# The prologue of a graph network layer: first tile's statistics ahead of the edge search, SyncE issuing its moves, search groups of 20 targets instead of 10

## The reference, cut to what matters

```python
h = jnp.maximum(_layernorm(x, axis=-1), 0.0)
agg = segment_sum(edge_attr_64, dst, 50000)
counts = segment_sum(ones, dst, 50000)
agg = agg / jnp.maximum(counts, 1.0)[:, None]
combined = jnp.concatenate([agg, h], axis=1)
out = x + relu(combined @ W1 + b1) @ W2 + b2
```

## Time and profile before

| what | value |
|---|---|
| median of 3 runs | 1390.73 us (1389.94 to 1390.91) |
| span of the profiled execution | 1387.8 us |
| TensorE busy | 98% of the span |
| VectorE busy | 92% |
| ScalarE busy | 59% |
| GpSimd busy | 52% |
| chain that ended last | PE 97% |

### The profile page before, as it was taken

The page is one execution under the profiler, slowest core; times in us unless marked ns, Lnnn a source line. Parts: engine busy times, 40 slices in busy tenths (PEclk is TensorE's granted clock), DMA queues, the critical chain, the costliest instruction groups (busy, mean ns, idle before and its releaser), DMA issues.

```text
span 1387.8 us, 31376 instructions
## 1 busy us (share of the span) xinstructions
PE 1356.9 (98%) x6882; PEld 1099.1 (79%) x6882; DVE 1276.5 (92%) x3267; ACT 818.9 (59%) x1672; POOL 727.1 (52%) x1004
## 2 busy tenths in 40 slices
PE   3899999999999999999999999999999999999998
PEld 1688888888888888888888888888888888888887
DVE  6789999999999999999999999999999999999996
ACT  3556565656566565656565656565666656565653
POOL 4554545555555555554545454555555555555451
PEclk7999999999999999999999999999999999999999
DMA  5575757576666666575757575766666666757572
GB/s 101 104 142 107 144 107 139 110 137 112 134 114 132 117 130 124 122 132 114 142 105 144 107 140 109 137 112 135 113 133 116 131 120 126 130 116 137 109 129 56
DMA packets 424646, 168.87 MB, mean 122 GB/s; under 512 B 323181, under 2 KB 424247, under 8 KB 424633
## 3 DMA queue, kind: packets, MB, share of 16 engines
q1 hardware_dynamic: 421348, 166.77, 62.7%
q10 hardware_dynamic: 3284, 1.97, 0.8%
HBM read 66.07 MB, written 51.20 MB: 85 GB/s over the span
## 4 chain that ended last, share of the span: by engine, by line
PE 97%; DVE 1%; DMA 1%; ACT 0%; POOL 0%; issue 0%; ACTq 0%; DVEq 0%; POOLq 0%
PE P L852 26%; PE P L832 13%; PE P L854 13%; PE P L834 13%; PE P L833 13%; PE P L842 7%; PE P L841 7%; PE PS L811 3%; PE PA L821 2%; DVE below L627 1%; DMA HQ<-HN 0%; DMA dst_a<-in_dst_dram 0%; DVE HT L667 0%; ACTq L256 0%; ACT HN L514 0%
## 5 line engine op out<-in xcount | busy, mean ns | idle before, releaser
L852 PE MATMUL P<-w_both,H_hi 128*128 128x512 f32 x1568 | 566.7, 399 | 0.1
L550 ACT ACTIVATE H_hi<-P 128x512 fp32r<-128x512 f32 x392 | 234.8, 599 | 381.1 <-PE P L842 380.5
L854 PE MATMUL P<-w_both,H_lo 128*128 128x256 f32 x1568 | 438.1, 279 | 0.0
L852 PEld LDWEIGHTS P<-w_both,H_hi 128*128 128x128 f32 x1568 | 294.3, 188 | 67.3 <-DVE H_lo L684 0.5
L832 PE MATMUL P<-HT_hi,w_hi 128*128 128x512 f32 x784 | 325.7, 415 | 16.4 <-DVE HT_lo L675 16.4
L406 POOL TENSOR_TENSOR XB<-X,b_row 128x1024 f32<-128x1024 f32 x98 | 235.0, 2398 | 198.3 <-DVE O L695 198.3
L834 PE MATMUL P<-HT_hi,w_lo 128*128 128x512 f32 x784 | 311.0, 397 | 0.0
L833 PE MATMUL P<-HT_lo,w_hi 128*128 128x512 f32 x784 | 310.6, 396 | 0.0
L684 DVE SCALAR_TENSOR_TENSOR H_lo<-P,H_hi 128x512 fp32r<-128x512 f32 x392 | 268.7, 686 | 32.6 <-ACT H_hi L550 19.7
L854 PEld LDWEIGHTS P<-w_both,H_lo 128*128 128x128 f32 x1568 | 294.5, 188 | 4.2
L667 DVE STREAM_TRANSPOSE HT<-HQ 128x512 f32<-128x512 f32 x196 | 212.7, 1086 | 18.4 <-DMA HQ<-HN 18.1
(11 more groups left out here) (73 smaller groups left out, 1512.4 us busy)
## 6 DMA issues: line engine op xcount, KB each, us to landing
X<-in_x_dram SPq DMA_DIRECT2D x98, 512.0 KB, 4.5
HQ<-HN SPq DMA_DIRECT2D x388, 128.0 KB, 4.1
out_dram<-O SPq DMA_DIRECT2D x97, 512.0 KB, 4.4
ER<-in_edge_attr_dram SPq DMA_DIRECT2D x392, 32.0 KB, 1.8
DW<-in_dst_dram SPq DMA_DIRECT2D x392, 0.5 KB, 1.9
w_raw<-in_L_gnn_W_dram ACTq DMA_DIRECT2D x4, 128.0 KB, 7.6
w_raw<-in_L_gnn_W_dram ACTq DMA_DIRECT2D x2, 256.0 KB, 8.2
HQ<-HN ACTq DMA_DIRECT2D x4, 128.0 KB, 4.8
```

Of the source, the lines that this page charges most:

```text
L550: act.activation(H1_hi[:, m, :], bank(m)[:], ACT.Relu).then_inc(s_1hi, 1)
L852: pe.matmul(out_bank(j)[:], H1_hi[:, m, rows], w2_both[:, m, :, :].rearrange("p a d -> p (a d)"), start=(m == 0), stop=False)
L854: last = pe.matmul(out_bank(j)[:, 0:D], H1_lo[:, m, rows], w2_both[:, m, 0, :], start=False, stop=(m == CH - 1))
```

## The change

On SP the load of the first tile's `X` is issued ahead of `dst_a`, and SP issues the four moves of tile 0, before it waits for `s_start`. On ACT `layernorm(0)` stands ahead of the five casts, and ACT issues no moves. On DVE the statistics of tile 0 stand ahead of the search instead of behind its first part. `GR` is 20 instead of 10, so that there are 10 groups and not 20.

```diff
-    EP, GR = 125, 10
+    EP, GR = 125, 20
...
+            load_x(0, 0)
             sp.dma_start(dst_a[:], dst.rearrange("(p r) -> p r", p=EP)).then_inc(s_dst, 16)
-            load_x(0, 0)
             sp.wait_ge(s_zero, 1)
...
             load_x(1, 1)
+            move(0, 0)
             sp.wait_ge(s_start, 1)
...
+            layernorm(0, 0)
             act.wait_ge(s_w[0], 16 * QN)
             act.activation(w1_hi[:], w1_raw[:], ACT.Copy).then_inc(s_whi, 1)
...
             act.activation(w2_both[:, :, 0, :], w2_raw[:], ACT.Copy).then_inc(s_whi, 1)
-            layernorm(0, 0)
-            act.wait_ge(s_ln, SUB)
-            into_quadrants(act, 0)
             layernorm(1, 1)
...
+            stat(0, 0, range(SUB))
+            aggregate(0, 0)
             dve.wait_ge(s_dst, 16)
             dve.tensor_copy(lasts[:], dst_a[:].rearrange("p (g r) -> p g r", r=GR)[:, :, GR - 1]).then_inc(s_srch, 1)
...
             dve.tensor_reduce(fall[:], falls[:], AX_X, ALU.max).then_inc(s_fall, 1)
 
-            stat(0, 0, range(SUB))
-            aggregate(0, 0)
             found = PS[:].rearrange("p a b -> p (a b)")
```

## The result

The changed kernel takes 1434.9 us (median of 5, 1430.14 to 1438.28), the kernel before in the same comparison 1390.91: a ratio of 1.031, 95% interval 1.029 to 1.033, or 44 us slower. The forecast was 1388.9, and rival 4, the slower one, said 1394.

The account below looks back on a forecast made before the run. PE's unbroken work was taken as the bound, so only its start could move. Flag 1.0 + SP's windows 0.8 + slack 0.4 - clock 0.4 = 1.8 us: 1390.73 becomes 1388.9 us, range 1387.0 to 1390.8.

Parts of the forecast that it names:

- rival 4: Prologue: `dst_a` lands late behind X, at 15.05 us, delaying the flag 4.5 us; 3.3 us slower, 1394.0 us; chance 0.05.
- the first: PE's stretch from 120 to 700 us, busy 580.00 of 580 us: the prologue can only move it forward, not shorten it.
- a limit of 108: Search with groups of 20: `longest` may reach 128 - 20 = 108, so the general way stays untaken.
- L: Landing of tile 0's `X`, issued at 0.95 us: forecast 7.85 us, bounds 6.05 to 8.75.
- `dst_a`: Its load, now behind X in the queue: landing forecast at 9.2 us, before DVE is free for the search at 9.6.
- The flag: End of the search, for which SP waits: up at L + 9.93 = 17.8 us against 18.78, 1.0 us earlier.
- "3.12": Term of the flag's forecast: us from `start_f` to the end of `flag_i`, 18.78 - 15.66 in the trace before.
- SyncE's windows: SP's `ER` loads behind the flag: 1.60 us apart instead of 2.39 without ACT's moves, giving 0.8 us back.
- PE's start: PE's first matmul, behind `layernorm(1)` on ACT: forecast at 26.6 us, 4.1 us earlier.
- Where the lines meet: Tile 0's step: DVE waits for tile 2's `X` and `DW`; `rel` moves 2.2 us earlier, including 0.4 us of slack.
- The clock: PE's stretch at 0.50 clock may fall partly behind the new start, 46.9 us: 0.4 us charged, bounds 0 and 1.7.
- The gain: Whole kernel: 1.8 us faster, median 1388.9 us; bounds -1.2 and 4.0 us.

Follow-up runs that it names:

- e12: The kernel before with HQ alone, the destination of the moves, shifted by 32 bytes: 1435.96 us, ratio 1.032.
- e1: The changed kernel with 9,824 unused bytes per partition behind `below`, so the buffers behind it lie where they lay before the change: 1390.28 us, ratio 0.9998.
- e4: The kernel before in its old order, with groups of 20 instead of 10: 1428.48 us, ratio 1.028.
- e3: The changed kernel with groups of 10 again, so the new order alone with every buffer where it was before: 1394.62 us, ratio 1.003.
- e9: The kernel before with 64 unused bytes per partition behind `below`, putting the streamed buffers at multiples of 256 bytes: 1385.38 us, ratio 0.9960.
- e8: e1 with GpSimd's low part of W1 made only after the flag and that of W2 behind `norm(1)`: 1388.78 us, ratio 0.9986 to the kernel before.
- e11: The kernel before with HN alone, the source of the moves, shifted by 32 bytes (HQ by 256): 1390.54 us, ratio 0.9998.
- e5: The changed kernel with 160 unused bytes per partition behind `below`, putting the streamed buffers at multiples of 256 bytes: 1386.97 us, ratio 0.9966 to the kernel before.
- e6: The kernel before with HN and HQ shifted by 32 bytes, buffers ahead in place, those behind shifted by 256: 1438.23 us, ratio 1.034.
- e7: The kernel before with X, XB, O and what lies behind HQ shifted by 32 bytes, HN and HQ keeping their remainder by 256: 1392.25 us, ratio 1.0011.
- e10: e8's order on GpSimd with e5's places, buffers at multiples of 256 bytes: 1384.11 us, ratio 0.9953 to the kernel before.

## Why the prediction was wrong

**The step that failed** is the first: "A change to the prologue cannot shorten that; it can only move it forward." It took the stretch from 120 to 700 us as fixed, and with it the durations of the transfers. But the diff also resized two buffers, and the buffers behind them moved. HQ, whose 256-byte pieces had begun at multiples of 64 bytes, now begins 32 bytes off. e12 makes that one shift in the kernel before and gets 1436.0; e1 undoes all shifts in the changed kernel and gets 1390.3; e4 and e3 put it on the line of the group size and not on the order. The group size was costed as ten compares and a limit of 108, its buffers not at all, and no rival covered it: rival 4 put the loss in the landing of `dst_a`.

**Why half a microsecond per tile costs 44 us.** The page of before held the warning: transposes waiting 18.1 us in all on the moves, in small portions. The round from transpose to transpose was as long as PE's 13.7 us for a tile: the transposes started on average 0.10 us after their moves had landed. A longer move could hide nowhere. The last move took some 0.55 us longer, 0.08 of it came out of that slack, and the mean round grew by 0.49 us. Over 97 tiles that is some 47 us, and the spans of the two profiled executions differ by 47.6 (1435.4 and 1387.8; the medians by 44). It is also the difference between 2,961 and 2,874 matmuls in 580 us. With the buffers at multiples of 256 bytes the transposes start 1.2 us after the landing, and behind the prologue none waits for a move (e9).

**The prologue's own steps**, which e1 isolates, since it is the changed kernel without the shift:

- L: 8.54 us instead of 7.85, within the bounds of 6.05 to 8.75. From issue to the first statistics are 7.6 us, which is 0.2 less than the 7.8 before and not 0.9; why `dst_a`'s 98 KB going ahead had cost so little is open.
- `dst_a`: right; the first compare follows the statistics at once, at 10.45.
- The flag: L + 9.93 would be 18.5; it came at 20.24. The missing 1.7 us are one term, "3.12" from `start_f` to the flag, carried over from a trace in which the cast (16.79 to 17.19) and `reach` were done before GpSimd's subtraction for W1 began at 17.69. The new order puts GpSimd's subtraction for W1 (16.04 to 18.39) beside the cast to `start_i`, which took 2.11 instead of 0.40 us. e3 shows the same with another operation and GpSimd's other subtraction; e8 removes the overlap and the cast is back at 0.40, the flag at 18.29. The Trainium skill, page "Advanced Engine Details and Errata", section "Mode Summary" under VectorE's performance modes, says that VectorE's second port to SBUF is shared with GpSimd, and that GpSimd's instructions and those of VectorE that use both ports block each other. The cast agrees with that, at 2.11 us beside the subtraction and 0.40 without it; that `reach`, held up as well, uses both ports in that sense no run shows.
- SyncE's windows: 1.70 and 1.61 us between the first `ER` instead of 1.73 and 2.39, as forecast (0.8 us).
- PE's start: 27.94 us, behind `layernorm(1)` on ScalarE, as forecast but 1.3 later, since `norm(1)` now waits for the second statistics, which stand behind the late flag.
- Where the lines meet: right as to the wait. VectorE waits 1.24 us for X of tile 2 and 1.28 for its `DW`. In e1 the flag is 1.5 us later than before, 0.75 come back in SyncE's windows and 0.4 from the slack; that leaves `rel` 0.3 late by the sum, and it starts at 47.53, 0.36 later than in the earlier trace rows. The time is the same as before within the interval.
- That the flag's line sets the time agrees with three kernels with equal places: 18.29, 20.26 and 24.63 us at the flag (e8, e1, e3) give 1388.8, 1390.3 and 1394.6 us. PE's first layer of tile 1 starts at 50.96, 53.01 and 57.38 us in them, and at 52.75 before. PE's own start does not order them: it is 28.37 us in e8 and 27.96 in e1.
- The clock: the stretch at 0.50 came later, as feared. In e1 it holds from 46.2 to 49.5 us, so the prediction's sign "low for long after 47 us" came up. What it costs there is open. At its old place it cost nothing, though 1.7 us had been the price of a whole one: in e9, whose prologue is that of before, the clock was 1.00 from 43.70 to 47.10 us, but PE was busy for only 2.44 of the 3.40 us, and the first layer of tile 1 started at 52.92.
- The gain: e8, with both surprises out, gains 2.0 us where 1.8 were forecast. That is in part luck: its flag came 0.5 us earlier than before and not 1.0, and its order on GpSimd is not that of the change.

## What to carry to other kernels

A change of a buffer's size is also a change of where every buffer behind it lies; look at the starts of the buffers that transfers of small pieces write, and pin them to multiples of 256 bytes instead of leaving them to what is declared ahead. Where an engine waits in small portions for the same transfer in half of the steps of a loop, the loop may be bound twice; a bound engine at 100% does not mean slack in the round beside it. When a step is moved, price it with what runs beside it in its new place, on VectorE and GpSimd above all.

## What the runs showed of the hardware that was not expected

- The start of the destination in SBUF matters for DMAs with pieces of 256 bytes. The last of a tile's four moves landed after 3.2 us with the buffers at multiples of 256 bytes, after 4.3 with HQ at 192 beyond one (a multiple of 64), and after 4.8 with HQ at 96 or 224 beyond (32 beyond a multiple of 64). Other remainders were not tried. The source did not matter between 192 and 224 beyond (e11); a source alone at a multiple of 256 was not tried, so which side gives the 3.2 us is open. The Trainium skill, page "DMA: Bandwidth & Descriptors", section "How a descriptor splits into AXI transactions", says that a transaction must start at a multiple of 256 bytes, and that a descriptor which starts elsewhere has bytes fetched that are not used; it says this of reading. By that rule, as an estimate, a piece of 256 bytes takes two transactions wherever it starts between two such multiples, and one at a multiple. The 3.2 us of e5 and e9 agree with it. But a start at 192 and one at 224 would then both take two, and e12 against before shows 45 us between them, so something more counts, and what it is stays open.
- Other transfers on the same DMA engines pay with it: X took 5.0 us in e6 and e12 at its old place, and 4.5 in e7 at a shifted one.
- VectorE's cast of 0.40 us and its `reach` of 0.55 us took 2.11 and 2.69 us beside GpSimd's subtraction of 128x1024, and ended 0.3 and 0.4 us after it. `end_f`, which reads PSUM, kept its 0.55 us beside it. It works the other way too: in e3 GpSimd's subtraction for W1, begun amid VectorE's compares, took 4.66 us instead of 2.35 and ended 2.5 us after the last of them.
- With the buffers at multiples of 256 bytes PE also did 2,967 to 2,970 matmuls in 580 us instead of 2,961 (e5, e9, e10), while never idle. A round took 13.68 us in the mean instead of 13.72, which over 97 tiles is 3.9 of the 4.1 us by which e9's span is shorter. Why it runs faster was not tested.
